# Half of the mask products of the next tile moved behind the first transposes of the present one

## The reference, cut to what matters

```python
q = layernorm(x) @ w_q.T + b_q;  k = ctx @ w_k.T + b_k;  v = ctx @ w_v.T + b_v     # 16 heads of 8
scores = einsum('bhqd,bhkd->bhqk', q, k)
scores = where(mask == 0, -1e9, scores) / sqrt(8)
x = x + tanh(g) * (softmax(scores) @ v @ w_o.T + b_o)
```

## Time and profile before

| | us |
|---|---|
| runs | 525.49 (median), 525.44, 529.74 |
| span of the profiled execution, first to last instruction | 522.8 |
| first layer's attention in it | about 15 to 178 |
| its expert layer | about 178 to 279 |
| second attention | about 281 to 432 |
| second expert layer | about 432 to 523 |

### The profile page before, as it was taken

The page is one execution under the profiler, slowest core; times in us unless marked ns, Lnnn a source line. Parts: engine busy times, 40 slices in busy tenths (PEclk is TensorE's granted clock), DMA queues, the critical chain, the costliest instruction groups (busy, mean ns, idle before and its releaser), DMA issues.

```text
span 522.8 us, 22052 instructions
## 1 busy us (share of the span) xinstructions
PE 446.0 (85%) x8481; PEld 325.6 (62%) x8481; DVE 367.3 (70%) x977; ACT 321.4 (61%) x764; POOL 273.2 (52%) x325
## 2 busy tenths in 40 slices
PE   2788899799978795999999689997897787889996
PEld 1455676566756585999984466665665565545554
DVE  5678788979787766355542779989898787544555
ACT  2355576566755773677754566767767467675653
POOL 2622534655474358888886435453444326534454
PEclk9999999999999988899999899999999999598999
DMA  7123444242111144665445010110031000000112
GB/s 204 50 55 114 109 124 122 61 113 69 45 39 37 40 98 104 89 94 73 48 37 153 2 43 5 43 34 23 3 84 35 21 4 3 2 1 6 41 51 68
DMA packets 50630, 30.69 MB, mean 59 GB/s; under 512 B 12384, under 2 KB 46944, under 8 KB 50528
## 3 DMA queue, kind: packets, MB, share of 16 engines
q1 hardware_dynamic: 37072, 18.54, 13.4%
q0 software_dynamic: 6640, 4.67, 7.0%
q10 hardware_dynamic: 6816, 6.07, 4.3%
HBM read 19.41 MB, written 9.85 MB: 56 GB/s over the span
## 4 chain that ended last, share of the span: by engine, by line
PE 45%; DVE 21%; issue 16%; POOL 7%; ACT 4%; DMA 3%; ACTq 1%; DVEq 1%; SPq 0%; POOLq 0%
DVE maxes L604 8%; PE T_ps L871 6%; PE S_ps L860 6%; POOL x_mid L1153 5%; PE A_ps L886 4%; PE m_H_ps L1464 3%; PE S_ps L854 2%; PE m_X_ps L1491 2%; PE m_T_ps L1504 2%; DVE prob L612 2%; PE f_H_ps L1205 2%; PE Q_ps L753 2%; PE Q_ps L841 2%; PE m_X_ps L1475 2%; PE m_X_ps L1447 2%
## 5 line engine op out<-in xcount | busy, mean ns | idle before, releaser
L604 DVE TENSOR_REDUCE maxes<-S_ps 128x8 f32<-128x512 f32 x128 | 87.5, 684 | 40.6 <-PE S_ps L860 40.6
L431 POOL TENSOR_TENSOR k_blk<-kT,col_a 128x512 f32<-128x512 f32 x64 | 67.9, 1070 | 82.1 <-ACT kT L492 57.9
L534 ACT ACTIVATE probT<-T_ps 128x512 f32<-128x512 f32 x128 | 76.1, 595 | 46.8 <-PE T_ps L871 46.0
L612 DVE TENSOR_TENSOR prob<-S_ps,maxes 128x512 f32<-128x512 f32 x128 | 88.5, 691 | 4.4
L871 PE MATMUL T_ps<-col_a,prob 128*128 128x128 f32 x512 | 83.1, 285 | 9.0 <-DVE prob L612 5.2
L871 PEld LDWEIGHTS T_ps<-col_a,prob 128*128 128x128 f32 x512 | 56.7, 143 | 46.9 <-issue 34.4
L1153 POOL DMA_INDIRECT x_mid<-f_out,f_rows x39 | 60.9, 1562 | 11.9 <-issue 10.7
L860 PE MATMUL S_ps<-k_blk,qT 32*64 32x256 f32 x1024 | 46.6, 411 | 5.3 <-DVE prob L612 4.5
L1018 DVE TENSOR_TENSOR f_hid<-f_H_ps,f_b 128x512 f32<-128x512 f32 x39 | 26.9, 691 | 33.3 <-PE f_Y_ps L1219 27.9
L886 PE MATMUL A_ps<-v_blk,probT 128*32 128x18 f32 x4096 | 48.4, 187 | 0.4 <-issue 0.4
L886 PEld LDWEIGHTS A_ps<-v_blk,probT 128*32 128x32 f32 x4096 | 41.8, 110 | 9.7 <-issue 8.9
(11 more groups left out here) (202 smaller groups left out, 881.2 us busy)
## 6 DMA issues: line engine op xcount, KB each, us to landing
f_w<-in_W ACTq DMA_DIRECT2D x16, 256.0 KB, 2.8
ctxT<-in_ctxT SPq DMA_DIRECT2D x12, 256.0 KB, 3.1
f_rows<-sorted_rows SPq DMA_DIRECT2D x39, 64.5 KB, 2.0
out<-m_final SPq DMA_DIRECT2D x32, 64.0 KB, 1.5
x_all<-in_x SPq DMA_DIRECT2D x6, 256.0 KB, 5.7
x_mid<-x_all SPq DMA_DIRECT2D x6, 256.0 KB
x_all<-x_mid SPq DMA_DIRECT2D x6, 256.0 KB, 3.6
ctxT<-in_ctxT SPq DMA_DIRECT2D x8, 128.0 KB, 3.1
```

What stands on the lines that cost most here:

```text
L431: nc.gpsimd.tensor_tensor(k_blk[:, t % 2, :, :, :], kT[:, g.at(R), t - g.first, :].rearrange("p (b k) -> p b k", b=2).unsqueeze(2).to_broa ...
L534: nc.scalar.activation(probT[:, t % 2, 4 * h:4 * h + 4, :], T_ps[:, :, :], ACT.Exp, scale=SCALE).then_inc(probT_ready, 1)
L604: nc.vector.tensor_reduce(maxes[:, t % 2, h, :, :], half_of(h), X, ALU.max).then_inc(max_ready, 1)
L612: nc.vector.tensor_tensor(prob[:, t % 2, heads, :].rearrange("p (r e) k -> p r e k", r=2), half_of(h), maxes[:, t % 2, h, :, :].unsqueeze( ...
```

## The change

The two mask products of `S_ps[0]` of tile t leave `score` and become a step of their own, `mask_first`, in slot t-2 at the place behind `turn_probs(0)` of tile t-1 and ahead of `turn_r` and `turn_x`. The two products of `S_ps[1]` stay in `score`. The waits on `mask_made` and on the cast go with the step, and it gets a wait on `shifted` at 2t-1, the first subtraction of tile t-1.

```diff
+            def mask_half(h, g, u):
+                for k in range(2):
+                    nc.tensor.matmul(S_ps[h][:, k, 0:HQ * S].rearrange("p (e k) -> p e k", k=S), w["ident_bf"][:, :],
+                                     mask_bias[:, g.at(R), u, :].unsqueeze(1).to_broadcast([P, HQ, S]),
+                                     start=True, stop=False, skip_group_check=True)
+
+            def mask_first(t):
+                g = GROUP_OF[t]
+                pe.wait_ge(mask_made, g.i + 1)
+                if t == 0:
+                    pe.wait_ge(r["casts"], 1)
+                wait(pe, shifted, 2 * t - 1)
+                mask_half(0, g, t - g.first)
+
             def score(t):
...
                 wait(pe, shifted, 2 * t)
                 if masked:
-                    pe.wait_ge(mask_made, g.i + 1)
-                    pe.wait_ge(r["casts"], 1)
-                    for h in range(2):
-                        for k in range(2):
-                            nc.tensor.matmul(S_ps[h][:, k, 0:HQ * S].rearrange("p (e k) -> p e k", k=S), w["ident_bf"][:, :],
-                                             mask_bias[:, g.at(R), u, :].unsqueeze(1).to_broadcast([P, HQ, S]),
-                                             start=True, stop=False, skip_group_check=True)
+                    mask_half(1, g, u)
...
-                     (turn_probs(0), tiles, shift(-1)), (turn_r, groups, settled(5, 8, short, later)), (turn_x, groups, turn_x_at)]
+                     (turn_probs(0), tiles, shift(-1)), (mask_first, tiles if masked else [], shift(-2)), (turn_r, groups, settled(5, 8, short, later)), (turn_x, groups, turn_x_at)]
```

## The result

The changed kernel took 521.08 us in the median (519.53 to 524.75), the kernel before 526.35 beside it (525.44 to 529.74): a ratio of 0.9895 [0.9852, 0.9938]. The forecast of 522.7 and its range hold the time, and 1.0% is at the edge of what can be told from no change. The profiled execution has a span of 517.7 us against 522.8, 5.1 less.

What follows compares the result with a forecast made beforehand. No engine alone bounds the kernel, but a chain passing between PE, DVE and issue. 2.2 + 0.2 + 0.3 = 2.7, called 2.8, off the median 525.49 gives 522.7; range 520.4 to 526.0, the forecast's own 521.8 to 524.2.

Steps and rivals of the forecast that it cites:

- Two products and one wait leave the path: Between second subtraction and scores: two products take 0.218 off, one wait instruction 0.06, together 0.28 us per tile.
- Where it counts: First attention, tiles where the chain waits before the masks: eight x 0.28 = 2.2 us, plus 0.2 at tile 31.
- the eight tiles: Tiles 2, 5, 7, 9, 10, 13, 17 and 21, where PE and DVE both idle; 0.28 us each.
- Where it does not: Tiles like 12 (PE queue without a gap) and 15 (DVE never idle) count nothing.
- the 0.22: Delay of `turn_r` and `turn_x` by the pair in gapless slots, a price only if ACT's copies cannot bear it.
- The new waits: `mask_first`'s waits hold only at tile 0, 0.1 lost to 0.5 gained; with tile 28, 0.3 us taken.
- Tile 28: The pair falls into PE's 1.9 us wait in `turn_r`, worth 0 to 0.22 us.
- The sum: First attention: 2.2 + 0.2 + 0.3 = 2.7, called 2.8 us with roundings; later stages move as a whole.
- No gain: Rival: time freed at one tile is given back at the next wait; 0 to 0.7 us remain, 525.2; chance 0.18.
- Not early: Rival: a wait of `mask_first` holds it until the second subtraction; 525.5; chance 0.02.
- Faster by holds that vanish: Rival: two holds of DVE's small operations by POOL products go away, 2.3 us more, 520.4; chance 0.09.
- Slower by DVE's small operations: Rival: earlier POOL products hold DVE's small additions, 1.15 us each; four more give 527.3; chance 0.13.

Runs made afterwards that it cites:

- e7: Changed kernel with the waits on `mask_made` and the cast put back into `score`, products still moved; 519.95 us, ratio 0.9896.
- e6: Kernel before with only those two waits taken out of `score`, all four mask products staying there; 521.97 us, ratio 0.9901.
- e2: Kernel before with the mask pair moved from tile 3 on only; 524.08 us, ratio 0.9963.
- e5: Changed kernel run again without any edit, 12 runs; 523.69 us, ratio 0.9942.
- e10: Changed kernel a third time without any edit, one run; 523.63 us.
- e1: Kernel before with the mask pair moved for tiles 0 to 2 alone; 524.39 us, ratio 0.9942.
- e3: Kernel before with unread identity products added to keep PE busy at the start; 524.47 us, ratio 0.9966.
- e12: Changed kernel with unread identity products keeping PE busy at the start, the same kernel as e4 run again; 521.62 us, ratio 0.9887.
- e11: e4 with one unread 512-column identity product put into PE's wait ahead of `turn_r` in the slot of tile 27; 519.28 us, ratio 0.9858.
- e4: Changed kernel with unread identity products added to keep PE busy at the start; 518.96 us, ratio 0.9847.

## Why the prediction was right, point by point

*Two products and one wait leave the path.* Right: 0.284 predicted, 0.283 to 0.286 measured, split by e7 and e6 into 0.219 and 0.067. The four loads run under the products, as taken. By the rule of the Trainium skill ("TensorE: Matmul & The Clock Gate", Part 3) that was weighed there, two products would be worth about 0.41 by the prediction's estimate; e7's 0.219 speaks against it for these loads.

*Where it counts.* All of the eight tiles gained 0.27 to 0.29 but tile 2, which gained 0.46, and tile 31 gained 0.18 as counted. Not counted were tile 8 (0.07) and, in e2 and e5, tile 19 (0.27 and 0.29). That tile's wait came and went with the pause ahead of it.

*Where it does not.* Tiles 12 and 15 show nothing in the first profile, and no tile there paid the 0.22. In e5 and e10 tile 12 lost 0.27; there the products ahead of the pair in that slot already ran 0.28 later, so it is not the pair's price.

*The new waits.* At the start (profile after, to hold against the earlier trace rows):

```profile
14.57 0.52 DVE L659 TENSOR_SCALAR mask_bias<-mask_in 128x128 bf16<-128x128 int32 x1
...
15.15 0.61 PE L845 MATMUL S_ps<-mask_bias,ident_bf 128*128 128x256 bf16 x2 [0.16 <-DVE mask_bias L659]
...
15.55 0.63 PE L794 MATMUL X_ps<-col_a,xn 128*128 128x128 f32 x2
...
16.16 0.58 PE L845 MATMUL S_ps<-mask_bias,ident_bf 128*128 128x256 bf16 x2
```

The pair waited for the bias and held `turn_x`, as said, and the second pair then had the end to itself: 0.39 gained of the bounds -0.1 to 0.5, where I took 0.2. Tile 28 gave 0.22 in e2, its upper end, where I took half.

*The sum.* 2.8 predicted; the loop gave 2.67 in the profile of the changed kernel, and e1 and e2 together 3.2. The size of the loop's gain was right, the way from it to the time was not whole. The end of the stage came 4.6 earlier where 2 to 3 was named as the sign, and by my own words the forecast is wrong where the time moves by over 3.2 us without a change in DVE's holds: the medians of the first set moved by 5.3, those of e5 and the kernel before beside it by 3.4. So that 521.08 lies in the range is in part luck: it is under the forecast's own 521.8, with a gain in it that no term of the sum named. At equal clock the 16 runs of the changed kernel (4, 11 and 1 at -5.1, -4.1 and -1.4) give -4.2 +- 0.5. What the sum left out is at tile 1: the pair at tile 0 puts work on PE earlier, and in three profiles of five PE then ran at its higher level 5 to 8 us sooner than in the kernel before, worth 1.8 to 2.0. On the average of the five that is about 1.2, and 2.7 to 3.2 + 1.2 = 3.9 to 4.4. That an early rate is worth some 2 us is shown by e3 (2.39 - 0.26 = 2.1). That the pair brings it, and that the share of three in five holds over the unprofiled runs, is an estimate; its fit to -4.2 proves little beside the 2 us of e6 that no stage accounts for.

*The rivals.* No gain: out, since each waiting tile kept its 0.28 to the end of the stage. Not early: out by the timeline of tile 9. Faster by holds that vanish: not seen. Slower by DVE's small operations: it was real at one tile. The lines of the small operations (min/median/max ns), after, to hold against the earlier trace rows, and the place:

```profile
L669 DVE TENSOR_TENSOR r_level<-r_same,row_constants x10: 175/192/1211, 81.1 to 195.4; 128x32 f32<-128x32 f32 x6, 128x16 f32<-128x16 f32 x4
...
L681 DVE TENSOR_TENSOR row_constants<-row_constants,rank_now x10: 166/167/978, 85.0 to 197.9; 128x8 f32<-128x8 f32 x10
...
L684 DVE CAST row<-row_all x10: 169/170/1653, 86.3 to 198.4; 128x4 int32<-128x4 f32 x6, 128x2 int32<-128x2 f32 x4
```

```profile
90.82 1.21 DVE L669 TENSOR_TENSOR r_level<-r_same,row_constants 128x16 f32<-128x16 f32 x1
90.93 1.06 POOL L431 TENSOR_TENSOR k_blk<-kT,col_a 128x512 f32<-128x512 f32 x1
```

L681 and L684 are unchanged. At tile 16 L669 (longest 0.240 before) now takes 1.21 and ends with POOL's product, while L673 behind it, which took 0.81 before, takes 0.17: 0.40 lost. The same 0.40 stands in eight of the nine profiles with the pair from tile 3 on (not in e12). The addition's recorded start is 0.11 ahead of the product's, so the prediction's picture, in which the one that starts later stands, does not cover this hold. Between 15 and 178 us, 7 operations last over 0.2 beyond the median of their line and shape, 5.2 us in all, against 8 with 5.9 before. The mechanism exists, its balance is 0.6 at most here.

*Left open.* Why the same start reaches the higher level early in some executions only. Why e6 gains more in the times than in its stage. What the pause in L814 is can be read further from the traces. It stands behind the same 29th product in most kernels, behind the 20th or 21st in three with instructions added ahead, and in e6, which has fewer wait instructions, behind the 5th product of the next line (L764): it goes by the place in the program. The page of the kernel before has a DMA queue for instructions (packets, MB, share of 16 engines):

```profile
q8 instruction: 70, 1.15, 0.9%
```

70 packets, 16 KB each. In all twelve profiles with the pause it ends 1.27 to 1.46 us after one of them is through, and so does e11's pause at 326.17 (1.28); in e4 and e11, without a pause here, the packet was through 2 to 3 us before the products of L814 began. So PE most likely stood until its next instructions had come. No run tried this, and why the packet comes earlier or later is open.

**The best version** is the changed kernel with PE busy at the start: 518.96 (0.9847 [0.98, 0.9894]) and 521.62 (0.9887 [0.9836, 0.9937]) in two sets of six, -6.2 at equal clock on the mean of both, 2 us under the changed kernel. The filler of e11 on top of it is not resolved.

## What to carry to other kernels

Work that does not depend on a wait belongs ahead of it in the queue; its worth is the pitch of its instructions (0.109), not their length (0.272), plus a wait instruction if one goes along (0.066), at each tile where both engines idle in turn. Where runs of one kernel lie up to 10 us apart, a gain of 3 us is read from the trace, event by event, and the times are compared at equal granted clock, which still left 2 us of e6 without a source. And when a span moves by more than the loop explains, look at how long identical instructions took in both profiles before a mechanism is sought.

## What was not expected of the hardware

- One more instruction with two semaphore waits in PE's queue costs 0.066 us behind the wait that is met last, though its own two had been met long before (e6, e7).
- PE's first rise to its higher level came at 24 to 26 us, at 17 to 19, or with denser work at the start at 13 to 15; the same program (changed kernel, e5, e10) showed both of the first two.
- A mean granted clock lower by 0.01 goes with 2.0 us, and it differs from 0.949 to 0.983 between runs of one kernel (e2).
- Thirteen pauses of PE of 0.63 to 2.35 us without a releaser each ended 1.27 to 1.46 us after a 16 KB packet of the instruction queue.
